# The first transformer layer with eight heads of 16 rows to a tile, instead of four heads of 32

## Chip, cores and metric

The kernel runs on one core of a Trainium2 chip, in one launch. The metric is device time in microseconds, the median of three runs. The core has TensorE (matmuls into PSUM), VectorE, ScalarE, GpSimd and the DMA engines; SyncE (SP in the profile) issues the transfers. All values are float32.

## The reference

A stream x of 4 batches with 512 positions and 256 channels, and a context of 4 x 64 positions with 192 channels, pass through four blocks:

```
x = mamba stack, 4 layers, on [64 context positions | 512 positions]     # L0
for each of three transformer layers (L1, L2, L3):
    h = layernorm(x);  x = x + W_o . concat_heads(softmax(q k^T * scale) v)   # q, k, v from h
    h = layernorm(x);  x = x + the same with k, v from the context
    h = layernorm(x);  x = x + feed forward(h)
```

All three transformer layers have 16 heads. In L1, the layer that is changed, a head has 256/16 = 16 channels (scale 16^-0.5), and Q, K and V have biases; in L2 and L3 a head has 64 channels.

## The kernel before

Everything is held transposed: channels on the 128 partitions, positions along the free dimension. The mamba stack runs first. Its innermost loop makes 32 steps for each batch and layer. In a step VectorE multiplies (L714) and scans (L722), GpSimd multiplies (L645), and TensorE sums into PSUM. Each step needs two rows of B and C, broadcast to all partitions. SP loads them into a ring of four buffers (BC, L256), each load waiting until GpSimd has finished with the buffer. In the last window SP first issues `prefetch`: the bias vectors (VEC) and the first layer's self-attention weights of Q, K and V into ARENA. Then it goes on with the BC rows.

A transformer layer l has self-attention, cross-attention and feed-forward. The arrays in DRAM hold every head padded to 64 rows or columns. `HPT[l]` heads share a tile of 128 partitions: 4 in the first layer (each 16 rows and 16 of zeros, HW = 32), 2 in the others. `NTL` is the number of tiles for a batch (4, 8, 8), `PPT` the number of pairs in a tile (2, 1, 1). `load_w` brings weights padded to 64 in one transfer, and in the first layer VectorE packs them to 32 in place (`pack`, L1531, six copies for a set of weights), once before self-attention and once at its end, before the cross-attention's setup. TensorE waits for these copies (s_wp).

Self-attention goes over 32 iterations `it` (4 batches x 8 pairs of heads), each with 4 query tiles of 128 positions, n = 4 it + i. Its loop body is written out for each engine in the same order, and semaphores connect them:

- TensorE: `scores` (L1141; for both heads of the pair one matmul, contraction over the head's rows, 128 x 512 into PSUM), `turn` (L1151, four transposes for each head), `values` (L1165, P times V, one PSUM bank for a tile of heads). For each tile it projects Q and K (`project`, L1120), once for a tile a quarter of V (`value_rows`, L1129), and twice for a batch the output (`finish`, L1175, NTL matmuls). All projections share one PSUM bank, B_J, which VectorE or ScalarE must empty before the next (s_pjf).
- VectorE: `shift` (L1578, negated maximum), `inverse` (L1584), `copies` (L1593, turned P from PSUM), `query` (L1570), `output` (L1600), the additions to the stream (L1605) and the layernorms.
- ScalarE: `exps` (L1399, exponential and its sum), `key` (L1382, K from PSUM with its bias), `value_rows` (L1390).
- GpSimd: the multiplication of P by the inverse sum (L1086), two for each n, three P buffers.

A float32 matmul is two passes, and each has its record in the trace. The two matmuls of a pair use different groups of rows (`scores`) or of columns (`values`) of the array, and run at the same time.

`cross_setup` projects K and V of the context into block matrices KB and VB (TensorE L1235 and L1240, ScalarE L1436 and L1447). TensorE does six of the setups before the last P times V and the rest after it. Then `cross_attention` runs 32 iterations: scores of a pair against KB (L1261), a row maximum and a subtraction (VectorE L1668, L1670), an exponential (ScalarE L1453), sum, reciprocal and product (VectorE L1677 to L1681), a turn (L1270, copied by ScalarE L1459) and P times VB (L1278). For each tile there is a Q projection (L1252, taken by VectorE L1657), and for each batch two output projections (`finish`, L1288, added by VectorE L1687).

## Time and profile before

| | |
|---|---|
| median of 3 runs | 5385.88 us (5373.51 to 5387.13) |
| profiled execution | 5388.29 us, span 5386.5 us |
| TensorE busy | 4888.6 us (91%) |
| VectorE busy | 3938.4 us (73%) |
| GpSimd busy | 2609.8 us (48%) |
| ScalarE busy | 2377.5 us (44%) |
| HBM read | 369.87 MB |

The span is one profiled execution; the time beside it includes what lies around the span. Busy time is a sum of the instructions on an engine; a matmul's end is modelled, so that a full TensorE is not TensorE at its peak. In the rows below a time from the span's start comes first, then a duration, both in us, then engine, line, operation, output <- input, shapes and, where merged, the number of records; the bracket is the idle time before it and what ended it. In the rows of busy time the columns are stretch, its length, then TensorE, its weight loads, VectorE, ScalarE and GpSimd with their numbers of instructions, then PEclk (the granted clock as a share of the full 2.4 GHz), DMA share and GB/s. The mamba stack takes the span until about 2439 us, the first layer's self-attention the time from there to 2982, its cross-attention until 3191, its feed-forward until about 3350.

### The profile page before, as it was taken

The numbers are of one execution on the slowest core, as the hardware profiler recorded it, in microseconds if no ns is written. First come the engines' busy times: TensorE is split into PE (matmuls) and PEld (weight loads), VectorE is DVE, ScalarE is ACT, GpSimd is POOL, SyncE is SP. The second block draws the span as 40 slices with busy tenths as digits, with TensorE's granted clock in tenths as the row PEclk, the third lists the DMA queues.
The fourth block names the chain that finished last, engine by engine and source line by source line (L and its number), as shares of the span: only waits on it lengthen the run. The fifth ranks groups of instructions, "written<-read, shape, count | busy, mean of one in ns | idle before, by whom it ended". The sixth has DMA issues, their size and how long they took to land.

```text
span 5386.5 us, 53903 instructions
## 1 busy us (share of the span) xinstructions
PE 4888.6 (91%) x18976; PEld 2662.3 (49%) x18976; DVE 3938.4 (73%) x3854; ACT 2377.5 (44%) x4086; POOL 2609.8 (48%) x1336
## 2 busy tenths in 40 slices
PE   7888988888888888877999889999998999999999
PEld 4455555555555555543555444555544445554444
DVE  4999999999999999985777653666645246665641
ACT  5555555555556555533434333433333233333321
POOL 2555555555555555555777112766600046665000
PEclk8999999999999999898999999999999999999999
DMA  2434343443343443430000010000001000001000
GB/s 106 143 143 147 132 152 144 146 147 143 143 147 145 140 143 144 151 126 13 1 1 24 16 39 1 1 1 1 24 24 38 3 1 1 1 1 48 0 1 16
DMA packets 94249, 376.65 MB, mean 70 GB/s; under 512 B 12960, under 2 KB 14240, under 8 KB 91040
## 3 DMA queue, kind: packets, MB, share of 16 engines
q1 hardware_dynamic: 93984, 373.19, 19.2%
q8 instruction: 157, 2.57, 0.2%
q14 instruction: 108, 0.88, 0.1%
HBM read 369.87 MB, written 3.28 MB: 69 GB/s over the span
## 4 chain that ended last, share of the span: by engine, by line
PE 45%; DVE 6%; ACT 1%; issue 1%; POOL 1%; DVEq 0%; ACTq 0%; POOLq 0%
PE PS L1141 6%; PE PS L1165 6%; PE PS L1151 6%; PE PS L1120 6%; PE PS L1328 5%; PE PS L1339 3%; PE PS L1129 3%; PE PS L1175 3%; PE PS L1288 2%; PE PS L1252 1%; PE PS L1240 1%; DVE PA L1670 1%; DVE CST L1668 1%; POOL PA L1086 1%; PE PS L1107 1%
## 5 line engine op out<-in xcount | busy, mean ns | idle before, releaser
L645 POOL TENSOR_TENSOR UH<-UH,BC 128x1152 f32<-128x1152 f32 x512 | 1344.5, 2626 | 1062.0 <-DVE U L714 1062.0
L1086 POOL TENSOR_SCALAR PA<-PA,INV 128x512 f32<-128x512 f32 x768 | 1190.9, 1570 | 595.8 <-DVE INV L1584 595.8
L392 PE MATMUL Y<-UH,ident_sb 128*128 128x512 f32 (+1 forms) x3072 | 1170.5, 526 | 240.9 <-POOL UH L645 135.9
L722 DVE TENSOR_TENSOR_SCAN UH<-DA,U 128x1152 f32<-128x1152 f32 x512 | 1307.2, 2553 | 21.7 <-ACT DA L583 4.3
L392 PEld LDWEIGHTS Y<-UH,ident_sb 128*128 128x128 f32 x3072 | 588.1, 203 | 863.2 <-issue 570.5
L1399 ACT ACTIVATE PA<-PS,NMX 128x512 f32<-128x512 f32 x768 | 519.4, 684 | 726.8 <-DVE NMX L1578 554.6
L583 ACT ACTIVATE DA<-DT,NEGA 128x575 f32<-128x575 f32 x1024 | 718.7, 763 | 101.1 <-DVE UH L722 69.8
L714 DVE TENSOR_TENSOR U<-DTX,BC 128x1152 f32<-128x1152 f32 x512 | 699.2, 1366 | 55.8 <-DVE DTX L700 7.1
L1593 DVE COPY VP<-PS 128x512 f32<-128x512 f32 x768 | 494.7, 685 | 280.3 <-PE PS L1151 259.1
L1578 DVE TENSOR_REDUCE NMX<-PS 128x2 f32<-128x1024 f32 x384 | 452.3, 1218 | 51.5 <-PE PS L1141 51.2
L1151 PEld LDWEIGHTS PS<-ident_sb,PA 128*128 128x128 f32 x3072 | 352.4, 142 | 241.4 <-issue 196.4
L1151 PE MATMUL PS<-ident_sb,PA 128*128 128x128 f32 x3072 | 415.7, 277 | 17.1 <-DVE VP L1593 15.7
L1141 PE MATMUL PS<-QK 64*128 64x512 f32 (+1 forms) x1536 | 389.2, 624 | 9.0 <-ACT PA L1399 6.5
L1165 PE MATMUL PS<-VP 128*64 128x256 f32 (+1 forms) x3072 | 376.8, 388 | 0.0
L1074 POOL TENSOR_TENSOR LSQ<-stream 128x512 f32<-128x512 f32 x21 | 26.6, 1266 | 689.9 <-DVE stream L1687 430.8
L1120 PE MATMUL PS<-HN,ARENA 128*128 128x512 f32 x640 | 318.0, 619 | 5.3 <-DVEq L1573 2.9
L1328 PE MATMUL PS<-HN,VP 128*128 128x512 f32 x640 | 288.6, 592 | 2.7 <-issue 2.7
L348 PE MATMUL PAIR<-HN,ARENA 128*128 128x288 f32 x984 | 265.7, 414 | 18.5 <-ACTq L526 13.2
L1165 PEld LDWEIGHTS PS<-VP 128*64 128x64 f32 (+1 forms) x3072 | 191.1, 128 | 130.7 <-issue 39.3
L348 PE MATMUL PAIR<-ARENA,DG 128*128 128x288 f32 x976 | 247.2, 405 | 0.0
L1722 DVE SCALAR_TENSOR_TENSOR QK<-PS,VEC,QK 128x512 f32<-128x512 f32 x64 | 48.0, 751 | 244.6 <-ACT QK L1497 244.6
L348 PEld LDWEIGHTS PAIR<-HN,ARENA 128*128 128x128 f32 x984 | 181.8, 195 | 62.2 <-ACTq L526 16.1
(157 smaller groups left out, 5419.8 us busy)
## 6 DMA issues: line engine op xcount, KB each, us to landing
BC<-bc_rows SPq DMA_DIRECT2D x512, 576.0 KB, 3.6
ARENA<-mamba_a SPq DMA_DIRECT2D x16, 1421.0 KB, 7.3
ARENA<-pair_w SPq DMA_DIRECT2D x6, 3072.0 KB, 10.5
WB<-mamba_b SPq DMA_DIRECT2D x16, 514.0 KB, 5.0
VP<-ff_w SPq DMA_DIRECT2D x2, 3072.0 KB
WO<-out_w SPq DMA_DIRECT2D x4, 1024.0 KB
stream<-x_t SPq DMA_DIRECT2D x2, 1024.0 KB, 10.2
VP<-ff_w SPq DMA_DIRECT2D x2, 1024.0 KB
```

What stands on the lines that cost most here:

```text
L348: mm = pe.matmul(to[0:out_rows, a, 0:HT], lhs, rhs(a), start=start, stop=stop)
L392: mm = pe.matmul(Y[:, a:b], IDENT[:, :], UH[:, SLOT[j], a:b], start=(s == 0), stop=(s == DS - 1), skip_group_check=True)
L583: ins = act.activation(DA[:, j % NDA, c * T + 1:(c + 1) * T], DT[:, bass.ds(par * (KI * T) + cc * T + 1, T - 1)], ACT.Exp, scale=NEGA[:, b ...
L645: pool.tensor_tensor(h, h, BC[:, j % NBB, 1, :].unsqueeze(1).broadcast_to([P, HK, T]), ALU.mult).then_inc(s_hc, 1)
L714: dve.tensor_tensor(u, x, BC[:, j % NBB, 0, :].unsqueeze(1).broadcast_to([P, HK, T]), ALU.mult).then_inc(s_u, 1)
L722: dve.tensor_tensor_scan(UH[:, SLOT[j], :], DA[:, j % NDA, :], U[:, 0:HC], 0.0, ALU.mult, ALU.add).then_inc(s_scan, 1)
L1086: pool.tensor_scalar(PR[:, n % 3, j, :], PR[:, n % 3, j, :], INV[:, n % 4, j:j + 1], None, ALU.mult).then_inc(s_ps, 1)
L1120: mm = pe.matmul(PS[:, B_J, :], w_tile(l, "qk".index(kind), t, k), HN[:, k, b * S0:(b + 1) * S0], start=(k == 0), stop=(k == KD - 1))
L1141: mm = pe.matmul(PS[:, B_S + 2 * (n % 2) + j, :], Q[r:r + HW[l], tt % 2, qt * P:(qt + 1) * P], K[r:r + HW[l], tt % 2, :], start=True, stop ...
L1151: mm = pe.transpose(PS[:, B_T + j, kt * P:(kt + 1) * P], PR[:, n % 3, j, kt * P:(kt + 1) * P], IDENT[:, :])
L1165: mm = pe.matmul(PS[r:r + HW[l], B_V, half * 256:(half + 1) * 256], VT[:, tt // QT % 2, kt, c:c + HW[l]], PT[:, hh % 2, kt, j, :], start=( ...
L1328: mm = pe.matmul(PS[:, 2 * (f % 2) + g, :], w1[:, k, c:c + P], HN[:, k, b * S0:(b + 1) * S0], start=(k == 0), stop=(k == KD - 1))
```

## The change

Eight heads share a tile in the first layer, 16 rows each, without padding rows. Layers 2 and 3 keep their form.

- Tiles of a batch in the first layer: 2 instead of 4. Q and K projections, Q projections of the cross-attention and the copies of all these are made half as often, and an output projection has two matmuls instead of four.
- The contraction of `scores` still takes 32 rows, which now hold two heads. `key` takes K out of PSUM twice, each time with a scale (MASK) and a bias (BKM) that are zero on every second head's rows, and `scores` reads the copy whose rows of the neighbour are zero. `head_of` gives the order: a pair is heads 0 and 2, then 1 and 3, 4 and 6, 5 and 7, so that the two of a pair stand in row groups 0 and 32, or 64 and 96.
- V of a position is 256 columns wide. It is written to VT with gaps (a head's 16 columns and 16 zeros, zeros first for odd heads), and `values` adds P times V of two neighbours up in the same 32 PSUM rows: `start` is set for the even head's first half alone.
- The packing copies go. `load_pairs` loads the heads to their places instead: 16 transfers with runs of 16 floats for Q and K and 2 for V, in place of one, both in `prefetch` and before the cross-attention. Biases and output weights take 8 transfers in place of 4, for each set.
- GpSimd zeroes VP once; VectorE makes the masks (`masks`: a sum over the identity matrix, and two products).
- Cross setup: 2 K setups instead of 4, and 4 V setups of 256 columns instead of 4 of 512, all six before the last P times V. Each K setup has 8 masked copies on ScalarE instead of 4, each V setup 8 instead of 4.

```diff
-HPT = (4, 2, 2)
+HPT = (8, 2, 2)
 GATED = (False, True, True)
 HW = tuple(P // h for h in HPT)
+RG = (32, 64, 64)
 NTL = tuple(NH // h for h in HPT)
 PPT = tuple(h // 2 for h in HPT)
+VW = tuple(min(512, NH * w) for w in HW)
+VPB = tuple(QT * NH * w // v for w, v in zip(HW, VW))
+VIT = tuple(NP // v for v in VPB)
...
+def more_values(l, it):
+
+    return it % VIT[l] == 0 and it // VIT[l] + QT < NB * VPB[l]
+
+
+def head_of(l, it, j):
+
+    p = it % NP
+    if HPT[l] == 2:
+        return 2 * p + j
+    return p // 4 * 8 + p % 4 // 2 * 4 + 2 * j + p % 2
...
+def load_pairs(sp, W, whp, s_w, l, c):
+
+    i = (2 * l + c) * NP
+    if HPT[l] == 2:
+        sp.dma_start(W[:, :, :, :, :].rearrange("p n k x m -> p n (k x m)"),
+                     whp[i:i + NP, :, :].rearrange("n p c -> p n c")).then_inc(s_w, 16)
+        return
+    of = whp[i:i + NP, :, :].rearrange("n p (k x m) -> p n k x m", k=KD, x=3)
+    for x in range(2):
+        for t in range(NTL[l]):
+            for k in range(KD):
+                to = W[:, t * PPT[l], k, x, :].rearrange("p (n j d) -> p n j d", j=2, d=HW[l])
+                for j in range(2):
+                    heads = of[:, t * PPT[l]:(t + 1) * PPT[l], k, x, j * HD:j * HD + HW[l]]
+                    sp.dma_start(to[:, :, j, :], heads).then_inc(s_w, 16)
+    for k in range(KD):
+        sp.dma_start(W[:, :, k, 2, :], of[:, :, k, 2, :]).then_inc(s_w, 16)
...
                         for j in range(2):
-                            r = row(l, it % NP, j)
-                            mm = pe.matmul(PS[:, B_S + 2 * (n % 2) + j, :], Q[r:r + HW[l], tt % 2, qt * P:(qt + 1) * P],
-                                           K[r:r + HW[l], tt % 2, :], start=True, stop=True)
+                            r, a = row(l, it, j), head_of(l, it, j) % 2 if HPT[l] == 8 else 0
+                            mm = pe.matmul(PS[:, B_S + 2 * (n % 2) + j, :], Q[r:r + RG[l], tt % 2, qt * P:(qt + 1) * P],
+                                           K[r:r + RG[l], tt % 2, a, :], start=True, stop=True)
                         mm.then_inc(s_sc, 1)
...
                         for kt in range(QT):
                             for j in range(2):
-                                r = row(l, it % NP, j)
-                                c = t % QT * P + r
-                                mm = pe.matmul(PS[r:r + HW[l], B_V, half * 256:(half + 1) * 256],
-                                               VT[:, tt // QT % 2, kt, c:c + HW[l]], PT[:, hh % 2, kt, j, :],
-                                               start=(kt == 0), stop=(kt == QT - 1), skip_group_check=True)
+                                r, h = row(l, it, j), head_of(l, it, j)
+                                c = h * RG[l] % 512
+                                shared = HPT[l] == 8
+                                mm = pe.matmul(PS[r:r + RG[l], B_V, half * 256:(half + 1) * 256],
+                                               VT[:, vg % 2, kt, c:c + RG[l]], PT[:, hh % 2, kt, j, :],
+                                               start=(kt == 0 and not (shared and (half or h % 2))),
+                                               stop=(kt == QT - 1 and not (shared and h % 2 == 0)), skip_group_check=True)
...
-                    pe.wait_ge(s_w, 16 * (2 * l + 1))
-                    pe.wait_ge(s_wp, START + 6)
+                    pe.wait_ge(s_w, w_loads(l, 0))
...
-                        act.activation(K[:, tt % 2, :], PS[:, B_J, :], ACT.Identity, bias=VEC[:, l % 2, c:c + 1]).then_inc(s_k, 1)
+                        if HPT[l] == 8:
+                            act.wait_ge(s_mk, START + 3)
+                            for a in range(2):
+                                ins = act.activation(K[:, tt % 2, a, :], PS[:, B_J, :], ACT.Identity, bias=BKM[:, a, t:t + 1],
+                                                     scale=MASK[:, a:a + 1])
+                            ins.then_inc(s_k, 1)
...
+                        if HPT[l] == 8:
+                            act.wait_ge(s_vz, START + 1)
+                            to = to.rearrange("p (n q d) -> p n q d", q=4, d=HW[l])[:, :, 0:4:3, :]
+                            act.activation(to, as_rows(l, PS[:, B_J, :]), ACT.Copy).then_inc(s_vn, 1)
...
-                def pack(l, c):
-
-                    dve.wait_ge(s_w, 16 * (2 * l + c + 1))
-                    w6 = W[:, :, :, :, :].rearrange("p (t q) k x m -> p t q k x m", q=2)
-                    for i, (q, of, to) in enumerate(((0, 64, 32), (1, 0, 64), (1, 64, 96))):
-                        if i:
-                            dve.wait_ge(s_wp, START + 6 * c + 2 * i)
-                        for x in range(2):
-                            dve.tensor_copy(w6[:, :, 0, :, x, to:to + HW[l]], w6[:, :, q, :, x, of:of + HW[l]]).then_inc(s_wp, 1)
+                def masks():
+
+                    dve.wait_ge(s_vec, VECS[0])
+                    dve.tensor_reduce(MASK[:, :], IDENT[:, :].rearrange("p (g a d) -> p a g d", a=2, d=HW[0]), AX.XY,
+                                      ALU.add).then_inc(s_mk, 1)
+                    dve.wait_ge(s_mk, START + 1)
+                    of = VEC[:, 0, V_BK:V_BV].rearrange("p (i q) -> p i q", q=PPT[0])[:, :, 0]
+                    for a in range(2):
+                        dve.tensor_scalar(BKM[:, a, :], of, MASK[:, a:a + 1], None, ALU.mult).then_inc(s_mk, 1)
...
-            sp.dma_start(ARENA[:, :].rearrange("p (n c) -> p n c", n=NP),
-                         a["pair_w"][0:NP, :, :].rearrange("n p c -> p n c")).then_inc(s_w, 16)
+            load_pairs(sp, ARENA[:, :].rearrange("p (n k x m) -> p n k x m", n=NP, k=KD, x=3), a["pair_w"], s_w, 0, 0)
```

TensorE at the second iteration (it = 1) of the first layer; QK are Q and K, ident_sb the turns, VP the P times V, HN,ARENA the projections of Q and K. Before:

```order
L1141 MATMUL PS<-QK 128x512 x4
L1120 MATMUL PS<-HN,ARENA 128x512 x2
L1151 MATMUL PS<-ident_sb,PA 128x128 x8
L1165 MATMUL PS<-VP 32x256 x8
L1120 MATMUL PS<-HN,ARENA 128x512 x2
L1151 MATMUL PS<-ident_sb,PA 128x128 x8
L1141 MATMUL PS<-QK 128x512 x4
```

and now:

```order
L1186 MATMUL PS<-QK 128x512 x4
L1196 MATMUL PS<-ident_sb,PA 128x128 x8
L1211 MATMUL PS<-VP 32x256 x8
L1196 MATMUL PS<-ident_sb,PA 128x128 x8
L1186 MATMUL PS<-QK 128x512 x4
```

The projections of the next tile are gone from this iteration; they stand at every fourth one.

TensorE at the end of the first layer's self-attention: CTXD are the setups of the cross-attention, ATT,WO the output projections, HN,ARENA the first query of the cross-attention. Before:

```order
L1151 MATMUL PS<-ident_sb,PA 128x128 x8
L1235 MATMUL PS<-CTXD,ARENA 128x256 x8
L1240 MATMUL PS<-ARENA,CTXD 128x512 x4
L1165 MATMUL PS<-VP 32x256 x8
L1240 MATMUL PS<-ARENA,CTXD 128x512 x4
L1175 MATMUL PS<-ATT,WO 128x512 x8
L1252 MATMUL PS<-HN,ARENA 128x512 x2
```

and now:

```order
L1196 MATMUL PS<-ident_sb,PA 128x128 x8
L1279 MATMUL PS<-CTXD,ARENA 128x256 x4
L1284 MATMUL PS<-ARENA,CTXD 128x256 x8
L1211 MATMUL PS<-VP 32x256 x8
L1222 MATMUL PS<-ATT,WO 128x512 x4
L1296 MATMUL PS<-HN,ARENA 128x512 x2
```

The V setups that stood between the last P times V and the output projections now stand ahead of it.

SP in the last window of the mamba stack; BC are the rows that the scan's steps wait for, VEC the biases, pair_w the weights:

```order
 L256 DMA BC<-bc_rows 128x1152 x4
-L855 DMA VEC<-vecs 128x12
-L856 DMA VEC<-vecs 128x23
-L859 DMA VEC<-vecs 32x48 x2
-L859 DMA VEC<-vecs 32x47 x2
-L1763 DMA ARENA<-pair_w 128x8x768
+L873 DMA VEC<-vecs 128x12
+L874 DMA VEC<-vecs 128x23
+L877 DMA VEC<-vecs 16x48 x2
+L877 DMA VEC<-vecs 16x47 x2
+L877 DMA VEC<-vecs 16x46 x2
+L877 DMA VEC<-vecs 16x45 x2
+L894 DMA ARENA<-pair_w 128x4x16 x16
+L896 DMA ARENA<-pair_w 128x8x128 x2
 L256 DMA BC<-bc_rows 128x1152 x11
```

Twenty-eight transfers stand ahead of the eleven BC rows instead of seven.

## Rows read from the trace of the kernel before

**Rows 1.** Busy time by stage: self-attention of the first layer, and its cross-attention.

```profile
2474.00:2982.00 508.00, 493.70 (x2779) 257.22 (x2776) 375.59 (x582) 209.25 (x554) 399.11 (x256) 0.97 0.02 7
...
3017.50:3190.60 173.10, 143.72 (x593) 81.28 (x592) 123.85 (x205) 57.99 (x93) 18.08 (x11) 0.97 0.07 25
```

**Rows 2.** Timeline, TensorE: scores at the start of five halves (start, us, engine, line).

```profile
2605.96 1.99 PE L1141 MATMUL PS<-QK 32*128 32x512 f32 x8
...
2611.94 1.99 PE L1141 MATMUL PS<-QK 32*128 32x512 f32 x8
...
2619.52 1.99 PE L1141 MATMUL PS<-QK 32*128 32x512 f32 x8
...
2628.89 1.99 PE L1141 MATMUL PS<-QK 32*128 32x512 f32 x8
...
2638.18 1.99 PE L1141 MATMUL PS<-QK 32*128 32x512 f32 x8
```

**Rows 3.** Timeline, start of the first layer: end of batch 0's norm, first projections.

```profile
2450.43 0.88 DVE L1562 TENSOR_SCALAR HN<-HN,VEC 128x512 f32<-128x512 f32 x2
...
2455.25 3.72 PE L1129 MATMUL PS<-ARENA,HN 128*128 128x512 f32 x4 [6.25 <-DVE ARENA L1531]
...
2467.85 1.98 PE L1120 MATMUL PS<-HN,ARENA 128*128 128x512 f32 x4 [0.73 <-ACTq L1392]
```

**Rows 4.** Timeline, copy of K and the first scores of its tile.

```profile
2505.13 0.69 ACT L1382 ACTIVATE QK<-PS,VEC 128x512 f32<-128x512 f32 x1 [2.26 <-PE PS L1120]
...
2505.91 1.99 PE L1141 MATMUL PS<-QK 32*128 32x512 f32 x8
```

**Rows 5.** Timeline, TensorE from the cross setup to the first cross query.

```profile
2984.65 9.24 PE L1235 MATMUL PS<-CTXD,ARENA 128*128 128x256 f32 x16 [2.29 <-issue]
...
3001.83 3.43 PE L1165 MATMUL PS<-VP 128*32 128x256 f32 x16
...
3009.41 3.70 PE L1175 MATMUL PS<-ATT,WO 128*128 128x512 f32 x8
...
3017.55 1.88 PE L1252 MATMUL PS<-HN,ARENA 128*128 128x512 f32 x4
```

**Rows 6.** Timeline, cross-attention: VectorE's maxima, output projection, query.

```profile
3060.78 0.68 DVE L1668 TENSOR_REDUCE CST<-PS 128x8 f32<-128x512 f32 x1
...
3064.45 0.68 DVE L1668 TENSOR_REDUCE CST<-PS 128x8 f32<-128x512 f32 x1
...
3068.84 0.68 DVE L1668 TENSOR_REDUCE CST<-PS 128x8 f32<-128x512 f32 x1
...
3074.64 3.70 PE L1288 MATMUL PS<-ATT,WO 128*128 128x512 f32 x8 [2.02 <-DVE stream L1687]
...
3080.09 0.81 DVE L1657 TENSOR_SCALAR PA<-PS,VEC 128x512 f32<-128x512 f32 x1 [3.82 <-PE PS L1252]
```

**Rows 7.** Timeline, SP's prefetch and VectorE's wait in the last mamba window.

```profile
2276.74 0.36 SPq L855 DMA_DIRECT2D VEC<-vecs  x1
...
2280.37 28.75 SPq L256 DMA_DIRECT2D BC<-bc_rows  x7
...
2292.47 1.37 DVE L714 TENSOR_TENSOR U<-DTX,BC 128x1152 f32<-128x1152 f32 x1 [3.12 <-DMA BC<-bc_rows]
```

**Rows 8.** DMA queues from 2440.6 to 2443.3 us: packets, MB, share of 16 engines.

```profile
q1 hardware_dynamic: 2143, 0.58, 97.9%
```

**Rows 9.** DMA queues from 2280 to 2290 us.

```profile
q1 hardware_dynamic: 1175, 3.55, 95.9%
```

**Rows 10.** Timeline, TensorE waits for VectorE's copy.

```profile
2702.78 1.22 PE L1151 MATMUL PS<-ident_sb,PA 128*128 128x128 f32 x8 [1.75 <-DVE VP L1593]
...
2703.93 3.20 PE L1141 MATMUL PS<-QK 32*128 32x512 f32 x8
...
2713.02 1.99 PE L1141 MATMUL PS<-QK 32*128 32x512 f32 x8
```

**Rows 11.** Busy time behind that wait: PEclk is the granted clock.

```profile
2704.00:2713.00 9.00, 9.00 (x41) 4.46 (x40) 5.58 (x10) 2.90 (x8) 8.75 (x6) 0.62 0.00 0
```

More of the change, by code:

```diff
@@ L830, in pj_uses @@
     for it in range(NITS):
-        tt, first, last = it // PPT[l], it % PPT[l] == 0, it % PPT[l] == PPT[l] - 1
+        tt, last = it // PPT[l], it % PPT[l] == PPT[l] - 1
         if last and tt + 1 < ALLT[l]:
@@ L838, in pj_uses @@
                 uses.append((kind, LN_AT[l][it - q]))
-        if first and tt + QT < ALLT[l]:
-            uses.append(("v", tt + QT))
+        if more_values(l, it):
+            uses.append(("v", it // VIT[l] + QT))
     return uses + [("o", (NB - 1) * KD + m) for m in range(KD)]
@@ L919, in as_rows @@
         def as_rows(l, ap):
+            ap = ap[:, 0:VW[l]]
             if HPT[l] == 2:
```

87 lines of the change are left out of this document (48 added, 39 removed).

## The prediction

> **What bounds the kernel now.** I read the busy time by stage first [rows 1]. The first transformer layer's self-attention lasts 508 us with TensorE busy for 493.7 of them; VectorE has 375.6 and GpSimd 399.1. So TensorE sets the end there, and GpSimd is next: its 256 multiplications of probabilities are those 399.1 us. In the cross-attention (173.1 us) TensorE has 143.7 and VectorE 123.9: neither is full, and each waits for the other.
>
> Then the timeline of TensorE, cut at the scores matmuls [rows 2]. Two query tiles of scores, their turns and P times V I call a half; there are 64 in a layer. A half with nothing else starts 5.98 us before the next (2605.96 to 2611.94). One with a value projection takes 7.58 (+1.60), one with the projections of Q and K 9.36 (+3.38), one with an output projection 9.29 (+3.31). TensorE runs these without a gap, so what leaves them shortens the layer, until GpSimd's 4 x 1.56 = 6.24 us for a half (399.1 / 64) holds.
>
> **The change part by part**
>
> Start. The value projections now wait for the packing copies and start at 2455.25, though batch 0 is normed at 2450.43 + 0.88 = 2451.31 [rows 3]. Packing goes; the masks that replace it (three tiny VectorE instructions) are wanted only by the first K, 10 us later, and hide behind the projections. So the start moves 3.9 us up. The four value projections take 12.6 us until the Q projection at 2467.85, each in turn TensorE and a copy on ScalarE. Both halve their columns, the latency stays: I take 8.0 for the four, another 4.6 saved, less about 0.7 for the second K [rows 4]. Together -7.5; bounds -3.5 (only the packing goes) and -9.
>
> Q and K. 16 tiles become 8. Of the 15 halves with a projection 8 turn into plain ones: 8 x 3.38 = -27.0.
>
> Values. 12 halves in the loop stream 256 columns instead of 512: half of 1.60, -9.6.
>
> Output projection in the loop. Two matmuls for each instead of four, 6 halves, half of 3.31: -9.9. Bounds for these three: nothing (GpSimd holds) and the full 46.5.
>
> K twice. The scores of a new tile start 0.78 us after ScalarE began on K, whose copy takes 0.69 [rows 4]. A second copy lies wholly on that path, 0.65 us more for 7 tiles: +4.6. Bounds 0 (if the next half catches up) and 5.
>
> Scores and P times V keep form and number. A pair still stands in row groups 0 and 32, or 64 and 96, so the two still run together; adding up in PSUM costs no instruction. The V copy writes 256 elements for 512 and has slack.
>
> End of self-attention to the first cross query [rows 5]. The setup waits 2.29 us after the last turn, for the packing: -2.3. The K setups are 9.24/4 = 2.3 us each, two go: -4.6. The four V setups take what lies between 2993.89 and 3009.41 without the 3.43 of the last P times V, 12.1; with 256 columns I take the K price, 9.2: -2.9. But nothing stands behind the last P times V now, so its copy is waited for: +1.1. Two output projections, from 3009.41 to 3017.55, lose 1.7 each: -3.4. ScalarE's K setups stay 16 instructions; its V setups double to 32, each of a quarter of the elements; I take them as done before TensorE is through with its projections. Sum -12.1; bounds -6 (the clock stays down longer) and -16.
>
> Cross-attention [rows 6]. An iteration with a query takes 4.39 us (3064.45 to 3068.84), one without 3.67; 8 queries go: -5.8. Where a batch ends, the second output projection starts at 3074.64, 3.70 long, then comes a query, and VectorE idles 3.82 us until 3080.09. It will be 1.85 long with no query behind it: the shift that started about 3081.4 comes at about 3078.3, of which 0.7 is counted already: 3 x 2.4 = -7.2. The last two lose 1.85 each: -3.7. Bounds for the three -10 and -20.
>
> Prefetch inside the last mamba window. This is what the change adds. SP issues 6 + 1 transfers at 2276.74 and then, from 2280.37, the BC rows that VectorE's scan needs; VectorE already waits 3.12 us for the first of them, until 2292.47 [rows 7]. Now 28 transfers stand before it: 10 for biases, 16 with runs of 64 bytes (8192 packets, 512 for each of 16 DMA engines) and two for V. Seven issues take 3.6 us now, so SP is through at about 2290.9. Behind that lie 1 MB of V and the BC rows' own 0.6 MB, so the rows land at 2296 to 2297.5: +5. The nearest row for a small packet is that of 256 bytes: in 2.7 us 2143 packets, nearly all of that size or less, took 97.9% of the 16 engines, 20 ns each [rows 8]. At that price the 64-byte runs need 512 x 20 ns = 10 us, beside the issuing. Dearest neighbour: packets of about 3 KB, 1175 of them at 95.9% in 10 us, 131 ns each [rows 9]. With p ns a packet the runs, begun at 2281.3, end 0.512p later, and some 5 us on (V, the BC rows, the landing) the scan can go: 0.512p - 6.1 us later than now, 4 at 20 ns and 61 at 131. I take 5, near the small packets; bounds 0 and 61.
>
> The Trainium skill, DMA: Bandwidth & Descriptors, section Specifications, says that below 512 B a transfer is read, modified and written. By that a 64-byte write would cost twice, 40 ns at the row's price, and the term would be 14 instead of 5; no run here shows such a packet yet.
>
> The same 18 loads of the cross weights are issued at iteration 27 of 32, over 60 us before their first use: nothing. Twice as many output-weight loads have 150 us.
>
> Drag. In runs of plain halves GpSimd's 6.24 exceeds 5.98; about 40 plain halves stand there afterwards, in runs of one to four between fuller ones that let GpSimd catch up. I take +4; bounds 0 and 15.
>
> Sum: -7.5 - 27.0 - 9.6 - 9.9 + 4.6 - 12.1 - 5.8 - 7.2 - 3.7 + 5 + 4 = -69.2. The profiled execution took 5388.3 us (span 5386.5), so 5319 in its terms; it lies 2.4 above the median of the timed runs, 5385.9, against which I predict **5317 us**.
>
> **The rivals**
>
> GpSimd or the chain scores, maximum, exponential, sum, multiplication, turn becomes the bound. For it: 78% busy now, 88% of what I leave (508 - 55 = 453). Against: 54 us of room remain, and fuller halves lie between. If half of the 46.5 is lost: 5340.
>
> TensorE's clock falls more often. For it: after a wait of 1.75 us for VectorE's copy [rows 10] the granted clock was 0.62 for 9 us [rows 11], partly the 1.2 GHz level, and the plain half in it took 2713.02 - 2703.93 = 9.09 us instead of 5.98, 3.1 lost; the change takes matmuls away, most in the cross-attention. Against: self-attention stays nearly gapless. One more fall per tile, 8 x 3.1, and a few in the cross-attention: 5345.
> The Trainium skill, TensorE: Matmul & The Clock Gate, section HAM oscillation, says that waits between bursts of matmuls let the gate close and that the way up is paid each time. The trace agrees, with one wait of 1.75 us and 3.1 us lost behind it.
>
> Small packets dear. At 86 to 90 ns the scan waits 39 us: 5350. It decides against the change from about 188 ns on: 0.512 x 188 - 6.1 = 90 us, more than 74.2 + 16. At 200 ns it is 96 us and 5408, slower. For it: the BC rows stand behind these packets in the same queues and VectorE is late there already. Against: 200 ns for 64 bytes when 256 cost 20 and 3 KB 131.
>
> The change doesn't do what it says: the paired scores no longer run together, as neighbours share a group of 32 rows. 64 x 1.7 = 109 us more, 5425. Against: a pair is heads 0 and 2, never 0 and 1.
>
> **How the numbers follow.** Forecast 0.60 (its own range 5303 to 5332), GpSimd or latency 0.15, clock 0.12, packets at 90 ns 0.08, packets at 190 or more 0.03, pairs apart 0.02. The range is 5300 to 5350. What a measurement here can tell from no change is 0.3%, 16 us. Only the last two cases are slower, and a mixture of the middle ones could end within 16 us: faster 0.91, same 0.04, slower 0.05.
>
> **What would show it.** Right: no copies into the weights; first value projection about 4 us after batch 0's norm; plain halves 6.0 to 6.2, value halves 6.8, Q/K halves 9.9 to 10.1 with a wait of some 0.6 us before the scores; GpSimd near 88% in self-attention; VectorE's wait at the prefetch 8 instead of 3.1 us. Wrong: that wait over 15 us; plain halves over 6.4; granted clock under 0.9 over the cross-attention.

## The result and the profile after

The changed kernel takes 5321.55 us, the median of 4 runs (5319.11 to 5326.33), beside 5386.51 for the kernel before in the same job. The ratio is 0.9885 (95% interval 0.987 to 0.9901): 1.15% faster. 5317 was predicted, with 5300 to 5350 as the range. The profiled execution's span is 5323.6 us for 5386.5, 62.9 less.

Cut at the same instructions in both traces, the difference lies here. In the first column of numbers is what the prediction said.

| stretch | predicted | before | after | difference |
|---|---|---|---|---|
| span's start to SP's first load of the transformer | +5 | 2438.94 | 2445.78 | +6.8 |
| that load to the first scores | -7.5 | 34.66 | 30.10 | -4.6 |
| first to last scores group of self-attention | -37.9 | 497.17 | 457.10 | -40.1 |
| last scores to the first cross query | -12.1 | 46.78 | 32.19 | -14.6 |
| cross query to the feed-forward part | -16.7 | 173.06 | 161.38 | -11.7 |
| the rest | 0 | 2195.9 | 2197.05 | +1.2 |

The busy time by stage, answering to [rows 1] (stretch, then busy us and instructions of TensorE, its weight loads, VectorE, ScalarE, GpSimd, then the granted clock, the DMA share and GB/s). The first row is the way to the first scores, the second the self-attention, the third its end with the setup, the fourth the whole cross-attention:

```profile
2445.80:2475.90 30.10, 20.52 (x34) 8.38 (x34) 10.71 (x18) 9.01 (x13) 10.43 (x4) 0.64 0.16 37
2475.90:2933.00 457.10, 436.59 (x2622) 234.61 (x2622) 360.77 (x554) 203.08 (x545) 387.68 (x250) 0.97 0.03 4
2933.00:2966.00 33.00, 26.98 (x123) 12.87 (x123) 10.77 (x17) 14.40 (x56) 10.53 (x7) 0.90 0.17 60
2965.17:3126.55 161.38, 124.04 (x529) 74.10 (x528) 117.63 (x197) 52.67 (x85) 16.97 (x10) 0.90 0.08 30
```

TensorE fills 436.6 of 457.1 us of self-attention; GpSimd comes close with 387.7 (85%), and has not taken over. In the start the granted clock is 0.64, and in the cross-attention 0.90, where it was 0.97 [rows 1]; "under 0.9 over the cross-attention" was one of the prediction's signs of being wrong, and this profile stands at its edge.

The timeline of TensorE shows the halves as [rows 2] did. The starts of the scores give a plain half 5.99, a value half 6.72 and a plain one 5.99 again:

```profile
2596.35 1.99 PE L1186 MATMUL PS<-QK 32*128 32x512 f32 x8
...
2602.34 1.99 PE L1186 MATMUL PS<-QK 32*128 32x512 f32 x8
...
2607.12 1.13 PE L1174 MATMUL PS<-ARENA,HN 128*128 128x256 f32 x4
...
2609.06 1.99 PE L1186 MATMUL PS<-QK 32*128 32x512 f32 x8
...
2615.05 1.99 PE L1186 MATMUL PS<-QK 32*128 32x512 f32 x8
2616.96 1.98 PE L1222 MATMUL PS<-ATT,WO 128*128 128x512 f32 x4
```

The output projection is two matmuls now (four records), and its half takes 7.58 (9.29 before). Q/K halves take 10.12 for 9.36; K's two copies answer to the one in [rows 4] and end in a wait of TensorE:

```profile
2530.30 1.45 ACT L1429 ACTIVATE QK<-PS,BKM,MASK 128x512 f32<-128x512 f32 x2 [2.25 <-PE PS L1165]
```
```profile
2531.85 1.99 PE L1186 MATMUL PS<-QK 32*128 32x512 f32 x8 [0.71 <-issue]
```

The start, answering to [rows 3]: the projections go at 2457.33, but all four, and the first after them, run slowly:

```profile
2446.67 3.78 PE L1148 MATMUL PS<-LSQ,ONES 128*128 128x512 f32 x4 [7.57 <-DVE LSQ L1597]
2452.36 2.88 PE L1152 MATMUL PS<-LSQ,ONES 128*128 128x512 f32 x4 [1.91 <-DVE LSQ L1607]
2457.33 2.05 PE L1174 MATMUL PS<-ARENA,HN 128*128 128x256 f32 x4 [2.09 <-DVE HN L1623]
...
2465.09 2.08 PE L1174 MATMUL PS<-ARENA,HN 128*128 128x256 f32 x4 [0.52 <-ACTq L1450]
2467.68 3.67 PE L1165 MATMUL PS<-HN,ARENA 128*128 128x512 f32 x4 [0.52 <-ACTq L1450]
2472.30 1.98 PE L1165 MATMUL PS<-HN,ARENA 128*128 128x512 f32 x4 [0.96 <-DVEq L1634]
```

The same two matmuls of 128x512 (four records) take 3.67 us for Q and 1.98 for K: the lower of the two clock levels, 1.2 GHz, against 2.4. Before, Q took 1.98 as well [rows 3].

The prefetch, answering to [rows 7]: SP issues 28 transfers before the BC rows, 16 of them in 9.45 us, and VectorE waits 10.30 for 3.12.

```profile
2277.39 3.67 SPq L877 DMA_DIRECT2D VEC<-vecs  x8
2281.10 9.45 SPq L894 DMA_DIRECT2D ARENA<-pair_w  x16
2290.59 1.27 SPq L896 DMA_DIRECT2D ARENA<-pair_w  x2
2291.90 11.97 SPq L256 DMA_DIRECT2D BC<-bc_rows  x4
```
```profile
2299.40 1.37 DVE L714 TENSOR_TENSOR U<-DTX,BC 128x1152 f32<-128x1152 f32 x1 [10.30 <-DMA BC<-bc_rows]
```

And one thing that the prediction did not have. VectorE's norm of a batch stands before its copies of turned probabilities, TensorE waits for these, and in three places the half behind runs at the low clock (0.64 from 2683.2 to 2692.0):

```profile
2675.01 1.84 DVE L1617 SCALAR_TENSOR_TENSOR HN<-HN,VEC,LRS 128x512 f32<-128x512 f32 x2
2676.77 1.51 DVE L1623 TENSOR_SCALAR HN<-HN,VEC 128x512 f32<-128x512 f32 x2
2678.21 2.34 DVE L1639 TENSOR_REDUCE NMX<-PS 128x2 f32<-128x1024 f32 x2
...
2681.01 1.28 DVE L1654 COPY VP<-PS 128x512 f32<-128x512 f32 x2
```
```profile
2677.23 1.92 PE L1211 MATMUL PS<-VP 128*32 128x256 f32 x16
2681.84 1.43 PE L1196 MATMUL PS<-ident_sb,PA 128*128 128x128 f32 x8 [2.69 <-DVE VP L1654]
2683.21 3.78 PE L1186 MATMUL PS<-QK 32*128 32x512 f32 x8
2686.92 1.97 PE L1196 MATMUL PS<-ident_sb,PA 128*128 128x128 f32 x8
2688.82 2.26 PE L1211 MATMUL PS<-VP 128*32 128x256 f32 x16
```

Those norm halves take 8.92, 8.71 and 8.71 us, and the ones behind 8.83, 9.09 and 9.09, where plain ones take 5.98. Before, [rows 10] and [rows 11] showed the same at a wait of 1.75 us; the norm halves took 7.76 or 7.77 there, and two of the ones behind 9.09, the third 5.99. (The norms of the batches 2 and 3 come early in the layer; their halves are followed by no such fall here.)

### The profile page after: what moved, and what is told of

Its sections match the earlier page's. It is cut to its first block, busy times and chain, and to the rows that moved or that the text cites. A ratio compares the mean times of both kernels' runs of the same rounds, so it can differ in the third digit from the quotient of the medians.

```text
span 5323.6 us, 53508 instructions
## 1 busy us (share of the span) xinstructions
PE 4809.0 (90%) x18808; PEld 2634.2 (49%) x18808; DVE 3922.3 (74%) x3821; ACT 2369.1 (45%) x4094; POOL 2613.6 (49%) x1337
## 4 chain that ended last, share of the span: by engine, by line
PE 45%; DVE 6%; ACT 2%; issue 1%; POOL 1%; DVEq 0%; ACTq 0%; POOLq 0%
PE PS L1186 6%; PE PS L1196 6%; PE PS L1211 6%; PE PS L1165 5%; PE PS L1372 5%; PE PS L1383 3%; PE PS L1174 3%; PE PS L1222 2%; PE PS L1332 2%; PE PS L1296 1%; DVE PA L1729 1%; DVE CST L1727 1%; PE PS L1305 1%; PE PS L1152 1%; PE PS L1284 1%
## 5 line engine op out<-in xcount | busy, mean ns | idle before, releaser
L714 DVE TENSOR_TENSOR U<-DTX,BC 128x1152 f32<-128x1152 f32 x512 | 699.2, 1366 | 63.0 <-DMA BC<-bc_rows 10.3
L1165 PE MATMUL PS<-HN,ARENA 128*128 128x512 f32 x576 | 287.7, 622 | 5.0 <-DVEq L1634 2.9
```

Of the source, the lines that this page charges most:

```text
L714: dve.tensor_tensor(u, x, BC[:, j % NBB, 0, :].unsqueeze(1).broadcast_to([P, HK, T]), ALU.mult).then_inc(s_u, 1)
L1165: mm = pe.matmul(PS[:, B_J, :], w_tile(l, "qk".index(kind), t, k), HN[:, k, b * S0:(b + 1) * S0], start=(k == 0), stop=(k == KD - 1))
```

## The experiments

All were timed beside the kernel before. Each starts from the changed kernel and computes the same output. The stage times are those of each profile, cut as in the table above; "layer" is first to last scores group of self-attention. A half is meant as in the prediction; the first two stand together, as their scores follow one another.

| kernel | median us | ratio to before, 95% | transformer starts | first value projection to scores | layer | cross |
|---|---|---|---|---|---|---|
| changed | 5321.55 | 0.9885 (0.987, 0.9901) | 2445.78 | 18.54 | 457.1 | 161.4 |
| e1 Q/K twice | 5349.47 | 0.9941 (0.9926, 0.9956) | 2447.01 | 20.45 | 482.0 | 158.8 |
| e2 K split | 5327.11 | 0.99 (0.9885, 0.9915) | 2446.62 | 17.81 | 464.3 | 156.0 |
| e3 norms moved | 5309.44 | 0.9868 (0.9852, 0.9884) | 2445.59 | 18.44 | 437.3 | 158.8 |
| e4 V wide | 5332.64 | 0.9909 (0.9893, 0.9926) | 2445.70 | 20.85 | 468.5 | 162.1 |
| e5 compact | 5320.85 | 0.9875 (0.9859, 0.9892) | 2439.70 | 20.45 | 457.9 | 161.4 |
| e6 spread | 5314.87 | 0.9865 (0.985, 0.988) | 2436.60 | 18.60 | 463.7 | 156.1 |
| e7 warm | 5317.81 | 0.9871 (0.9857, 0.9886) | 2444.92 | 13.08 | 459.0 | 158.8 |
| e8 add first | 5313.43 | 0.9862 (0.9848, 0.9877) | 2445.62 | 18.38 | 457.0 | 149.1 |
| f1 four together | 5280.31 | 0.9809 (0.9795, 0.9822) | 2435.29 | 13.09 | 436.6 | 149.0 |
| f2 and K split | 5274.78 | 0.9796 (0.9782, 0.9809) | 2436.24 | 12.41 | 432.1 | 148.9 |
| f3 changed, again | 5324.12 | 0.9889 (0.9875, 0.9902) | 2448.82 | 18.52 | 457.0 | 156.0 |

Except for "Q/K twice" the single edits move the median by at most 12 us, and their intervals overlap with that of the changed kernel; only "Q/K twice", "four together" and "and K split" lie clear of it. What a single edit did is therefore read from its stages, of which there is one profile each. How far a stage moves by itself shows where an edit doesn't touch it: the start (first value projection to scores) takes 18.4 to 18.6 in five such profiles and 20.45 in "Q/K twice" and "compact"; the layer takes 457.0 to 459.0, and 463.7 in "spread"; the cross-attention takes 156.0 to 162.1.

**Q and K twice.** Theory: TensorE's own instruction time is the layer's time.

```diff
-                        for k in range(KD):
+                        for k in [*range(KD)] * (2 if l == 0 and tt else 1):
```

> From tile 1 on, the Q and K projections of the first layer are computed twice (each 4 extra matmuls of 512 columns overwrite the same PSUM bank with the same values). Theory A (TensorE's own instruction time is what the layer lasts): all of the added matmuls show. 7 tiles x 2 projections x 4 matmuls at 0.213 to 0.216 us are 12.0 us, so scores to scores goes from 457.1 to about 469 and the Q/K halves from 10.12 to about 11.8. Rival B (GpSimd, busy for 387.7 of the 457.1 us, or the chain from maxima to probabilities, has taken over the pace): the extra matmuls fall into TensorE's waits; under 4 us longer, and the plain halves behind the Q/K halves get shorter.

The layer got 24.9 us longer. All seven Q/K halves went from 10.12 to 13.56, the first two halves, which the edit leaves alone, took 0.95 more together, and the others stayed within 0.15:

```profile
2527.37 3.70 PE L1165 MATMUL PS<-HN,ARENA 128*128 128x512 f32 x8
...
2533.72 3.70 PE L1165 MATMUL PS<-HN,ARENA 128*128 128x512 f32 x8
```

The 12 us in the expectation are an error of mine by a factor of 2: eight passes take 3.70 and four 1.98, so one is 0.43 us, not 0.21. With 0.43 the sum is 7 x 8 x 0.43 = 24.1. All of it shows, and nothing is hidden by waits for GpSimd or the chain to the probabilities: theory A, and the rival falls.

**V projections wide.** The columns alone are put back.

```diff
+                                to = PS[:, B_J, :].rearrange("p (n j d) -> p n j d", j=2, d=32)
+                                w = W[:, :, k, 2, :].rearrange("p n (j d) -> p n j d", j=2)[:, :, :, 0:32]
```

> The value projections of the first layer are left at 512 columns (16 real columns and 16 of zeros per head), as before the change; the copy out of PSUM takes the 16. All else is as in the changed kernel. Theory A (halving a matmul's columns halves its time on the path): every value half goes from 6.72 to 7.58, 12 of them in the layer, so 457.1 + 10.3 = 467.4. In the start the four value projections take 3.2 us longer, but if the low granted clock in the start comes from the shorter projections, the Q projection is back at 1.98 for 3.67 and the start is only 1 to 2 us longer. Rival B (the low clock in the start comes from what stands before the projections, the waits between the statistics matmuls): the wide projections run at the low level too, and the start grows by 3.4 to 7 us. Rival C (columns do not matter for the value half, its length is VectorE's or ScalarE's): the halves stay at 6.7.

Nine of the twelve value halves grow by 0.85 or 0.86 (6.72 to 7.58, 7.7 to 8.56, 8.49 to 9.34). The third half of the layer grows by 0.60, one with statistics by 0.70, and the one that waits for a norm not at all: it stays at 8.71, and TensorE's wait in it falls from 1.64 to 0.79. Together that is 9.0 us of the 11.4 that the layer lost; most of the rest, 2.8, lies in the norm halves and those behind them. Rival C falls. In the start the clock came up two projections earlier than in the changed kernel:

```profile
2465.73 3.78 PE L1178 MATMUL PS<-ARENA,HN 128*128 128x512 f32 x4 [0.52 <-ACTq L1453]
2470.03 1.98 PE L1178 MATMUL PS<-ARENA,HN 128*128 128x512 f32 x4 [0.52 <-ACTq L1453]
2472.53 1.98 PE L1165 MATMUL PS<-HN,ARENA 128*128 128x512 f32 x4 [0.52 <-ACTq L1453]
```

The Q projection is at 1.98 as A had it, but two wide projections ran at the low level and the first took 2.72, and the start grew by 2.3, between the two expectations. That sum decides nothing, as the unaltered start of "Q/K twice" grew by 1.9 on its own. The place of the fall says more: wide projections did not keep it away, and in the changed kernel the clock was low before the first projection began:

```profile
2454.00:2457.30 3.30, 1.24 (x2) 0.00 (x0) 2.32 (x5) 2.16 (x4) 2.23 (x1) 0.50 0.21 51
```

So the short projections are not what brought the low level about.

**Warm.** The waits before the projections are the next suspect: three matmuls into an unused bank, in waits that stand there anyway.

```diff
+                pe.wait_ge(s_w, w_loads(0, 0))
+                warm(1)
...
+                warm(2)
```

> Three added fp32 matmuls of 512 columns into an unused PSUM bank stand in TensorE's waits before the first value projections: one behind the sums of the mean, two behind those of the variance. Theory A (the low granted clock through the value projections and the Q projection comes from the waits of 7.57, 1.91 and 2.09 us around the short statistics matmuls): the Q projection takes 1.98 for 3.67 and some of the value projections 1.0 for 2.08, so from the first value projection to the first scores it takes 14.5 to 17 for 18.54. Rival B (a few more matmuls do not bring the clock back): 18.5 as before, or up to 1 us more where they are still running when the projections could start.

```profile
2449.37 1.07 PE L1398 MATMUL PS<-ARENA,ONES 128*128 128x512 f32 x2
...
2453.68 1.88 PE L1398 MATMUL PS<-ARENA,ONES 128*128 128x512 f32 x4
2456.47 1.10 PE L1174 MATMUL PS<-ARENA,HN 128*128 128x256 f32 x4 [0.92 <-DVE HN L1630]
...
2463.04 1.98 PE L1165 MATMUL PS<-HN,ARENA 128*128 128x512 f32 x4 [0.52 <-ACTq L1457]
```

Every projection runs at 2.4 GHz: 1.10 to 1.13 for 2.05 to 2.08, Q 1.98 for 3.67. From the first value projection to the first scores it is 13.08 for 18.54, 5.5 less and more than I expected; the granted clock from 2445.0 to 2469.5 is 0.91, where it was 0.64. "Four together" has the same 13.09. (Each of the three matmuls shows as two records.)

**Norms moved.** The norm's VectorE work goes one half earlier, and before VectorE's copies.

```diff
-    at = {1: job(0, 0, 2), 4: job(0, 0, 3)} if l == 0 else {3: job(l, 0, NB - 1)}
-    at.update({NP * (b + 1) + 3: job(l, 1, b) for b in range(NB - 1)})
+    at = {1: job(0, 0, 2), 5: job(0, 0, 3)} if l == 0 else {3: job(l, 0, NB - 1)}
+    at.update({NP * (b + 1) + (3 if l else 5): job(l, 1, b) for b in range(NB - 1)})
```

> In the first layer the normalization of a batch is moved by one half, into the half that projects Q and K, and its VectorE instructions are placed ahead of the copies of Q and K's neighbours instead of behind them. Theory A (the three halves of 8.7 to 8.9 us in which VectorE normalizes are long because that VectorE work no longer has a 10 us half to hide in, and the low granted clock in the half behind each is the result of that wait): those halves fall to 6 to 7.5, the halves of 9.09 behind them to 6.0, and the layer is 12 to 17 us shorter. Rival B (the added statistics matmuls of the norm cost TensorE this time wherever they stand): the same sum shows up in the Q/K halves, which go to 12 to 13, and the layer stays within 4 us of 457.

The layer is 19.8 us shorter, more than A's 12 to 17. The Q/K halves stay at 10.12 with the norm inside, all 32 plain halves are 5.97 to 6.33, and behind the first two no half is at the low clock:

```profile
2475.60:2912.90 437.30, 426.65 (x2622) 230.80 (x2622) 355.15 (x550) 203.11 (x545) 388.18 (x250) 0.99 0.03 5
```

TensorE is busy 426.7 us here and 436.6 in the changed kernel, with the same 2622 instructions: 9.9 us of its busy time was slow clock, the other 9.9 were waits. Rival B falls. GpSimd's 388 us are 89% of this layer, and TensorE waits for it once, for 0.70 us.

Not all of this is a gain. The last norm has moved behind the last scores, out of the layer as I cut it, and holds TensorE up there:

```profile
2921.48 1.94 PE L1196 MATMUL PS<-ident_sb,PA 128*128 128x128 f32 x8 [2.56 <-DVE VP L1654]
```

From the last scores to the first cross query it takes 34.93 us for 32.19, so 17.1 of the 19.8 are left. The median gained 12.1; the profile is that of the fastest of four executions (5304.61 to 5317.21 us).

**K split.** The even heads' scores wait for the first copy of K alone.

```diff
-                        pe.wait_ge(s_k, START + TBASE[l] + tt + 1)
+                        if HPT[l] == 8 and head_of(l, it, 0) % 2 == 0:
+                            pe.wait_ge(s_k0, START + tt + 1)
+                        else:
+                            pe.wait_ge(s_k, START + TBASE[l] + tt + 1)
```

> The scores of even heads wait for the first copy of K alone, those of odd heads for the second. Theory A (the second copy, 0.65 to 0.76 us, lies wholly on the way from the K projection to the scores): the seven Q/K halves go from 10.12 back to about 9.4 and the layer is 7 x 0.7 = 5 us shorter (452.0 for 457.1), the start 0.7 shorter too. Rival B (the longer Q/K half comes from something else, such as PSUM banks still held by the maxima): the halves stay at 10.1 and nothing changes.

The seven halves are 9.45, as A had it, and the start is 0.7 shorter; yet the layer is 7.1 us longer. The first tile change shows why. The half behind it went from 7.01 to 7.68, so 9.45 + 7.68 is the 10.12 + 7.01 of before: VectorE, with a norm in that half, sets the end of the two. TensorE's wait in it grew from 0.99 to 1.66 us, and then the clock fell:

```profile
2541.38 1.23 PE L1200 MATMUL PS<-ident_sb,PA 128*128 128x128 f32 x8 [1.66 <-DVE VP L1657]
2542.53 2.88 PE L1190 MATMUL PS<-QK 32*128 32x512 f32 x8
2545.34 1.97 PE L1200 MATMUL PS<-ident_sb,PA 128*128 128x128 f32 x8
2547.23 3.42 PE L1215 MATMUL PS<-VP 128*32 128x256 f32 x16
```

The half that begins with these scores took 9.08 for 5.99. In the eight profiles in which this wait was 0.99 or 1.00 us it took 5.98 or 5.99 each time, so these 3.1 us belong to the split.

The norm halves and those behind them took 19.07, 19.33 and 19.09 a pair for 17.75, 17.80 and 17.80 (4.1 more), and the third half of the layer 10.55 for 6.98 (3.6 more), at a granted clock of 0.62. I found no wait there that the changed kernel does not have too, and kernels without the split show the same: four pairs of 18.96 to 19.37 in "V wide" and "warm", a third half of 10.28 in "spread" and of 11.21 in the kernel before. That these 7.7 us come from the split is not shown; without them the layer would be 0.6 shorter.

**The prefetch.** Two edits tell the length of the packets from the place in SP's queue. "Compact" lays the first layer's Q and K out without their padding in memory, so that 4 transfers bring a set in place of 18. "Spread" keeps all 28 transfers with their 64-byte runs, but issues them two at a time behind the later BC loads of the window.

```diff
-    for x in range(2):
-        for t in range(NTL[l]):
-            for k in range(KD):
...
+    for t in range(NTL[l]):
+        sp.dma_start(W[:, t * PPT[l], :, 0:2, :].rearrange("p k x m -> p k (x m)"),
+                     of[:, t * PPT[l], :, 0:2, :].rearrange("p k x m -> p k (x m)")).then_inc(s_w, 16)
```

> Q and K of the first layer are laid out without their padding in the weights as they lie in memory, so that a set of pairs comes in 4 transfers with runs of 1 KB and more in place of 18 transfers, 16 of them in runs of 64 bytes. Issue of a set on SyncE's queue falls from about 10.7 to about 2.5 us, and no packet of 64 bytes is left. Theory A (the last Mamba window is 7 us later because the many issues and small packets stand ahead of the broadcast load on SyncE's queue): VectorE's wait for that load falls from 10.30 to 3.1 or less and the transformer starts 7 to 9 us sooner, at 2437 to 2439 for 2445.8; about 5313. Rival B (the wait is for the load's own transfer behind the 2 MB of weights, however they are cut): the wait stays above 8 and the start above 2444.

```diff
                         load_state(n, j)
+                        if not prep and j > NBB:
+                            for _ in range(2):
+                                if later:
+                                    later.pop(0)()
```

> The same transfers of the same 64-byte runs as in the changed kernel, but issued two at a time behind the broadcast loads of the last Mamba window, from the second on, and not all ahead of them. Theory A1 (what costs is the place on SyncE's queue: some 15 us of issues ahead of a load that is due): the wait of 10.30 goes to under 2 us and the transformer starts 8 to 10 us sooner, although the packets stay as small. Theory A2 (what costs is the packets of 64 bytes, which hold the DMA engines): the loads between them each come late instead, the window gets no shorter, and the start stays within 3 us of 2445.8.

Compact: VectorE's wait is 3.23 and the transformer starts 6.1 us sooner, a little less than expected. The median is that of the changed kernel (5320.85); in the profile the start then took 20.45 for 18.54. Spread: VectorE has no wait left at the BC rows of this window, and the transformer starts 9.2 us sooner, with the same small packets. So A1 holds and A2 falls: the cost was the place on SP's queue. The three kernels with this edit start the transformer at 2435.29 to 2436.60, the eight with the prefetch of the changed kernel at 2444.92 to 2448.82. The median gained 6.7; in the profile 6.6 us of the 9.2 were lost in the layer again, in halves at the low level that the changed kernel does not have (the third took 10.28, a Q/K half 13.47), and 5.3 gained in the cross-attention. Neither stage was touched by this edit.

**Add first.** In the cross-attention the addition to the stream becomes VectorE's first work of its iteration.

```diff
+                        if l == 0 and NP + 5 <= at < NITS and at % NP in (5, 6):
+                            add(at // NP - 1, at % NP - 5)
```

> In the cross-attention of the first layer the addition to the stream of a finished batch is VectorE's first work of its iteration and not behind the shift of the scores. Theory A (the second output projection of a batch waits 3.55 us for that addition, and with it the clock falls): the iterations at a batch's end take about 4 to 5.5 for 7.15, three batches, and the cross-attention 6 to 10 us less than the 156 to 161 of the runs so far. Rival B (the maxima and shifts of the next scores are now late by the 0.7 to 1.5 us of the addition and TensorE waits for those instead): the batch's end gets shorter by under 2 us each, and the cross-attention stays above 156.

The changed kernel has, at a batch's end, a wait of 3.55 us and an output projection at low clock:

```profile
3088.18 1.88 PE L1332 MATMUL PS<-ATT,WO 128*128 128x512 f32 x4
3095.80 3.63 PE L1332 MATMUL PS<-ATT,WO 128*128 128x512 f32 x4 [3.55 <-DVE stream L1746]
```

With the edit there is no wait between the two:

```profile
3045.56 1.88 PE L1332 MATMUL PS<-ATT,WO 128*128 128x512 f32 x4
...
3049.70 1.98 PE L1332 MATMUL PS<-ATT,WO 128*128 128x512 f32 x4
```

The cross-attention takes 149.1 us, under everything from 156.0 to 162.1 that the variants without the edit took, and 149.0 and 148.9 in the two kernels below. Theory A.

**Together, and once more alone.**

> Four edits that each gained alone, together: the norms of the first layer one half earlier (layer -19.8), the prefetch spread behind the broadcast loads (start of the transformer -9.2), three matmuls in the waits of the first norms (start -5.5), the stream addition first in the cross-attention (-7 to -12). Theory A (the places are apart and their costs add up): 5321.5 - 19.8 - 9.2 - 5.5 - 9 = about 5278, range 5272 to 5284. Rival B (the falls of TensorE's granted clock turn up elsewhere once their old places are filled): half of the gain or less, 5290 to 5305, with halves of 9 to 10.5 left in the layer's trace.

> The same four, and the scores of even heads wait for the first copy of K alone. Theory A (the 7.1 that the layer lost with this edit alone were falls of the granted clock, at halves 2, 9 and behind the norms, set off by waits that the other edits have now taken away): the layer is 7 x 0.67 = 4.7 and the start 0.7 shorter than with the four edits, about 5273. Rival B (releasing the even heads' scores early costs the layer time in itself): it is 5 to 8 longer than with the four.

> The changed kernel itself, unaltered, beside the other two on the same chip. If its stages repeat, the layer's scores to scores lasts 457.1 within 0.3 and its norm halves are 8.7 to 8.9 again; the cross-attention, which took 161.38 in this kernel and 156.0 to 162.1 in variants that leave it alone, tells what part of such differences is chance: if it comes out at 156 or 159 here, chance alone moves that stage by 3 to 5; if at 161.4, the variants' differences have causes in them.

The four edits give 5280.31, and with the K split 5274.78; theory A each time. The first is 2 us from its sum. In the second the split brought 4.5 us in the layer and 0.7 in the start; the stretch behind the last scores took 1.5 more. The slowest execution with the split (5275.02) is faster than the fastest without it (5277.34). The layer's busy time in this last one:

```profile
2460.20:2892.30 432.10, 426.15 (x2620) 230.44 (x2620) 355.01 (x549) 203.49 (x546) 387.86 (x250) 0.99 0.03 5
```

TensorE is busy for all but 6 us of 432.1. This version is 2.04% faster than the kernel before (interval 1.91 to 2.18), and by the medians of the same job 49 us faster than the changed kernel; the two intervals against before lie apart. It is the best of all that was run.

The changed kernel again: 457.0 in the layer, with the same norm halves to 0.01, so the layer repeats here. But its cross-attention took 156.03 for 161.38, and its transformer started 3.0 us later. One and the same kernel thus moves by 5 us in the cross-attention between two profiles, which is as much as I had missed there:

```profile
2968.12:3124.15 156.03, 119.54 (x530) 72.98 (x528) 117.52 (x197) 52.63 (x85) 16.98 (x10) 0.93 0.08 31
```

TensorE's busy time is 4.5 us less with the same instructions, at a granted clock of 0.93 for 0.90; its waits are 0.9 less.

## Why the prediction was right

**The bound** was read rightly. TensorE's instructions set the time of the self-attention: what was taken away came off one for one, and what was put back came back: 24.1 us of 24.1 with Q and K twice, and 9.0 of 10.3 with V wide, where a wait for VectorE took up part of one half.

**Q and K, values, output projections.** Eight Q/K halves less at 3.38 are -27.0. A value half fell by 0.86 where I took 0.80, 12 of them make -10.3 (-9.6 predicted). An output half fell by 1.71 where I took 1.65, 6 are -10.3 (-9.9 predicted).

**K twice** costs 0.76 in each of seven halves, +5.3 for +4.6. That it lay nearly all on the path is shown by the split, which made these halves 0.67 shorter.

**Drag by GpSimd** was put at +4 and is nothing: plain halves are 5.98 as before. My 6.24 per half for GpSimd was a busy time from which I had made a limit; the layer later ran with GpSimd at 388 of 432 us, and plain halves still took 5.98.

These make -42.3, and the layer shows -40.1. The missing term is the norm of a batch. Four of the five norm halves take 4.1 us more than their kind of half should (8.92, 8.71 and 8.71 for 7.76 or 7.77, and one with a value projection 8.71 where 8.47 - 0.86 = 7.61 was due), and behind the last a half went to the low clock, 3.1. Against it stand 3.4 in the layer's third half, which had been slow before (11.21) and now is not (6.98), and some 1.6 in the half of the first norm (7.01 for 7.77) and in those with statistics. The 3.4 are luck: whether the third half falls to the low level changes from kernel to kernel with no edit there ("spread" has it again). I looked at four kinds of halves [rows 2] and not at the one with a norm. It could have been seen in [rows 10]: that wait for VectorE's copies was a norm half. The rival "TensorE's clock falls more often" asked for one more fall per tile and did not come in that form; it came once more behind a norm, in the cross-attention (0.90 for 0.97), and in the start, where the warm kernel prices it at 5.5 us.

**Start**: -4.6 for -7.5 (the terms as I gave them, 3.9 and 4.6 less 0.7, add up to 7.8). The step "Both halve their columns, the latency stays: I take 8.0 for the four" failed by clock. Four projections took 10.35 us (2457.33 to 2467.68), since none of them ran at 2.4 GHz, and Q took 1.7 more. With the clock up (the warm kernel) the four take 6.57 (2456.47 to 2463.04), less than my 8.0. The step was sized at a granted clock that the stretch did not have.

**Tail**: -14.6 for -12.1. The wait for the packing is gone, and the K setups of two groups take 2.48 together, 1.2 each, where I had taken 2.3 from a stretch of the trace at the lower clock. What I called free was not: TensorE waited 2.77 us for ScalarE's copies of K.

```profile
2944.07 2.48 PE L1279 MATMUL PS<-CTXD,ARENA 128*128 128x256 f32 x8
...
2953.61 2.37 PE L1284 MATMUL PS<-ARENA,CTXD 128*128 128x256 f32 x4 [2.77 <-ACT KB L1496]
2955.91 3.52 PE L1211 MATMUL PS<-VP 128*32 128x256 f32 x16
```

**Cross-attention**: -11.7 for -16.7 in this profile, -17.0 in the second one of the same kernel. The sum is right in one and too large in the other by what the clock does there. I had put the second output projection of a batch at 1.85 us; the three took 2.76, 2.94 and 3.63 in the first profile and 1.98, 2.81 and 2.97 in the second. The wait ahead of them grew as well, to 3.5 or 3.6 us from the 2.02 of [rows 6]. "It will be 1.85 long with no query behind it" was true of the instruction at the full clock and left out both.

**Prefetch**: +6.8 for +5. SP was through at 2291.90 for the 2290.9 predicted, and the rows took 7.5 us from there, where I had allowed 5.1 to 6.6. The small packets were not dear: 7728 packets, nearly all of 64 bytes, took 52.4% of 16 engines over 10 us, 0.524 x 160 / 7728 = 10.8 ns each, half of the 20 ns of [rows 8].

```profile
q1 hardware_dynamic: 7728, 0.48, 52.4%
```

What counts is SP's 0.59 us for each issue (9.45/16), and that the load that VectorE needed stood behind it. The prediction had both parts in it, but its bounds ran over the price of the packets and not over the place in the queue. The Trainium skill, DMA: Bandwidth & Descriptors, section Specifications, says that below 512 B a transfer is read, modified and written. From that I had made 40 ns for such a packet, and this step was wrong by itself: the 256-byte packets of [rows 8] are below 512 B too, so whatever such a write costs is in their 20 ns already. The trace shows no 40 ns, and no run here tells what part of the 10.8 is that of the read and modify.

The total came out this near by luck, as the misses cancelled: the self-attention and the tail gained 4.7 more than predicted, the start, the prefetch and the cross-attention 9.7 less, and the rest of the program took 1.2 more.

How a wait and the fall behind it go together in this layer can be counted over the nine profiles of the changed kernel and of the variants that leave the norms in place, and that of the kernel before. After a wait of 2.69 or 2.70 us for VectorE's copies the half behind was at the low level in 27 of 27 cases; after one of 1.63 to 1.76 in 4 of 13; after one of 0.99 or 1.00 in none of 8.

What stays open: why the clock falls after some of the middle ones and not after others, and why in the third half of some kernels with no such wait ahead; why the transformer starts 3 us apart in two profiles of one kernel; whether the kernel before, with its norms moved in the same way, would gain as much as the changed one did, which was not tried.

## What to carry to other kernels

Where one engine fills a stage, price removed work by that engine's instructions, but go through every kind of iteration, above all the rare one in which another engine has extra work: taking matmuls away takes its cover away. A wait of TensorE costs more than itself when the granted clock falls behind it (here a wait of 2.7 us, then some 3 us in the next half), so look for what makes it wait, and put the second engine's extra work into TensorE's longest iteration; useless matmuls in a wait can pay too. Before adding transfers to a queue, look for the load behind them that is due soonest and issue them after it, few at a time. Before you explain a few us in one stage by an edit, look how far that stage moves in profiles in which nothing of it was changed.

## What the runs showed of the hardware

- Three matmuls of 512 columns in waits before four short projections brought these from 2.08 to 1.13 us each, and the stretch 5.5 us in all.
- Removing 0.67 us from seven iterations lengthened a wait from 0.99 to 1.66 us and put the half behind it at the low clock (9.08 us for 5.99); with the norms moved, so that the wait was gone, the same edit made the layer 4.5 us shorter.
- Behind a wait of 2.7 us in an else full TensorE the next half (5.98 us at full clock) was at the low level 27 times of 27; behind 1.63 to 1.76 us, 4 times of 13; behind 0.99 or 1.00, never in 8.
- A 64-byte packet from HBM took 10.8 ns of a DMA engine, one of mostly 256 bytes ([rows 8]) 20; the issue of such a transfer held SP's queue for 0.59 us.
- In one stage and one kernel two executions differ by 5.4 us (cross-attention 161.38 and 156.03), of which 4.5 are TensorE's busy time at another granted clock (0.90 and 0.93).
